# Moving the last-but-one half's outputs in a fused transformer/Mamba/recurrence kernel to other engines, with more PSUM banks for the last z projection

## The chip, the cores and the metric

One core of one Trainium2 chip runs the whole program. The metric is the device time of one execution in microseconds (us), lower is better. TensorE (PE) multiplies matrices into PSUM, VectorE (DVE), ScalarE (ACT) and GpSimd (POOL) work elementwise, and SyncE (SP) issues most of the DMAs. GpSimd reaches SBUF alone; the other two reach PSUM as well.

## The reference, cut to what matters

```python
x = x + ga * dilated_attention(adaln(x))          # layer 0
x = x + gb * fp6_ffn(adaln(x))
h = adaln(x)
x_branch, z = split(h @ in_proj_w)                # layer 1: Mamba block, D_INNER 512, 16 states
# causal conv over x_branch, silu, x_proj -> B_t, C_t, dt
for t in time: s = exp(dt*A)*s + dt*B_t*x; y = s @ C_t
x = x + ga * ((y + D*x_branch) * silu(z)) @ c_proj_w
h = adaln(x)                                      # recurrence over the BATCH index, 1024 tokens side by side
for b in 0..3: c = sig(h[b]@wf.T + c@uf.T + bf)*c + sig(h[b]@wi.T + c@ui.T + bi)*tanh(h[b]@wc.T + c@uc.T + bc)
x = x + gb * tanh(h @ wo.T + c_final @ uo.T + bo) # needs the c of the last batch
```

x is (4, 1024, 256) in float32.

## The kernel before, in words

The 4 x 1024 tokens are cut into 8 halves of 512 tokens (half 2b and 2b+1 are batch b). Each half has 32 scan steps, 256 in all: a step handles two of the 16 states of one of the four 128-channel blocks (`kd`). In a step GpSimd makes the input of the step (L1914), ScalarE two decays (L1254), VectorE the scan (L1691) and then its product with C (L1697), and TensorE adds two tiles with an identity matmul into PSUM bank Y (L874), from where VectorE takes the gated sum once per eight steps (L1677, `dve_gate`). While half h is scanned, the rest of half h-1 (z projection of the next half, c_proj, layer norm, gates, `px`) and the attention and convolution of half h+1 run between the steps.

The order on each engine is written out at build time. Every chain is a generator that yields a due time in steps (`TIMES`), and `in_time` merges the chains with the scan parts quarter by quarter; a chain part that is due comes ahead of the scan part of that quarter. After that the order in each engine's queue is fixed, and semaphores do the rest. `after(6)` is step 224, the first step of half 7.

Three places matter here. (1) **z of half 7**, steps 229 to 234: four blocks, each a matmul group (`pe_z`, L712), a tanh by ScalarE (L1142) and a product by VectorE (`dve_z`, L1421), all four through the single bank Y0; each next block's matmul waits for VectorE's product of the one before (`S.z_ev`). (2) **Outputs of the even half of all four batches**, steps 252 to 256: when half 6 has given the last c, TensorE makes `om` in banks X0 and X1 (L859). `dve_final` adds the bias (L1603) and adds `om` to the four stored `px` tiles (L1605) in the order `OUT_ORDER` = 3, 0, 1, 2; ScalarE takes four tanh (L1212), GpSimd multiplies the four by the gate row (L1887), and VectorE adds them to the four residual tiles (`dve_sum`, L1615: two behind the last scan steps, two in `dve_last`). SyncE stores each. `pe_last` makes the c_proj of half 7 for the first three channel blocks early (L747, steps 254 and 254.5); the second part uses bank X0 and so waits for the fourth `om` addition (`S.fin_add`). (3) **Behind the last scan**: `dve_gate`, last c_proj block, layer norm 4, transposes (L458), gates (L720, L728), the new c (L1639 to L1648 on VectorE), `om` of the odd halves (L784), and their outputs. `dve_last` adds the bias row to three stored tiles in that stretch (L1632).

Of the kernel before, what the change touches and what calls it, by code (L numbers as in the profile page):

```python
# [13 lines left out]
P = 128  # L14
# [88 lines left out]

OUT_ORDER = (3, 0, 1, 2)
LAST_CPROJ, LAST_GATE, LAST_PX, LAST_OM = (Y0, X0), (X1, 0, 1, 2, 3, Y), (Y0, Y), 0
# [9 lines left out]
         "modrow_step", "masks_bf", "wq_step", "wq_mm", "ffnT", "negA", "c0", "halved", "dt_mm",  # L115
         "sp_first", "first_dt", "first_row", "sums_open", "wo_gated", "ffn_gated", "cp_gated"]
ATTENTION = ["q_mm", "k_mm", "q_ev", "k_ev", "v_mm", "s_mm", "nmax", "e_ev", "rsum", "v_ev",
# [5 lines left out]
RECURRENT = ["cp_mm", "cp_tmp", "resA", "g_mm", "g_ev", "g_sig", "px_mm", "px", "c_f", "i_g", "c_new"]  # L123
END = ["om", "om_bias", "fin_add", "fin_tanh", "fin_gate_pool", "fin_gate_dve", "fin_sum", "out"]
LN = namedtuple("LN", "stats aggr step nb hn mm out")
# [13 lines left out]
def build(nc, d):  # L139
    with ExitStack() as ctx:  # L140
# [270 lines left out]
        def sp_final():  # L411
            yield after(G - 2) + 31
            for n, b in enumerate(OUT_ORDER):
                sp.wait_ge(S.fin_sum, n + 1)
                sp_out(0, b)

            sp.wait_ge(S.fin_gate_pool, B + 2)
            sp_out(1, 0)
            for n, b in enumerate((1, 2)):
                sp.wait_ge(S.fin_sum, B + n + 1)  # L420
                sp_out(1, b)
            for q in range(2):
                sp.wait_ge(S.fin_sum, B + 3 + q)
                sp.dma_start(d["out"][B - 1, TH:T, :].rearrange("(p j) e -> p j e", j=JH)[:, 2 * q:2 * q + 2, :],
                             two(xrs[1][B - 1], q)).then_inc(S.out, 16)
# [60 lines left out]
        def pe_first():  # L486
# [43 lines left out]
            for k in range(KE):  # L530
                for jo in range(2):
# [6 lines left out]
            pe.matmul(ps[:, Y, :], identF[:], wqT[:, 0:2, :, :].rearrange("p h k v -> p (h k v)"), start=True, stop=True,  # L538
                      skip_group_check=True).then_inc(S.sums_open, 1)
            pe_idle(9)  # L540
# [169 lines left out]
        def pe_z(h, kd):  # L710
            for k in range(KE):
                x = pe.matmul(ps[:, Y0, :], inw[:, k, DI + kd * P:DI + (kd + 1) * P], hB3[:, k, :],  # L712
                              start=(k == 0), stop=(k == KE - 1))
            x.then_inc(S.z_mm, 1)
# [24 lines left out]
        def pe_last():  # L739
# [11 lines left out]
            for q in range(2):  # L751

                yield t + 30 + q / 2
                if q == 0:
                    pe.wait_ge(S.gated, 4 * g + KD - 1)
                    pe.wait_ge(S.cp_gated, B)
                    pe.wait_ge(S.px, 2 * g)
                else:
                    pe.wait_ge(S.fin_add, B)
                for kd in range(KD - 1):  # L760
                    c_proj(kd, q)
# [29 lines left out]
        def pe_after(g):  # L791
# [19 lines left out]
            for kd in range(KD):  # L811
                yield t + TIMES["pe_after"]["z"][kd]
                if kd:
                    pe.wait_ge(S.z_ev, 4 * (g + 1) + kd)
                elif g >= 0:
                    pe.wait_ge(S.cp_tmp, 2 * g + 2)
                else:
                    pe.wait_ge(S.xc, 4)
                if kd == 0:
                    pe.wait_ge(ln["ln3"].out, 2 * (g + 1) + 2)  # L820
                pe_z(g + 1, kd)
# [308 lines left out]
        def act_after(g):  # L1130
# [6 lines left out]
            for kd in range(KD):  # L1137
                yield t + TIMES["act_after"]["z_tanh"][kd]
                if kd == 0 and g >= 0:
                    act.wait_ge(S.cp_mm, 2 * g + 2)  # L1140
                act.wait_ge(S.z_mm, 4 * (g + 1) + kd + 1)
                act.activation(sz[:, kd, :], ps[:, Y0, :], ACT.Tanh, scale=0.5).then_inc(S.z_tanh, 1)  # L1142
                if kd == 1 and g >= 0:
                    for j in (0, 2):
                        yield t + TIMES["act_after"]["hnA"][j // 2]
                        act.wait_ge(ln["ln4"].nb, g + 1)
                        if g:
                            act.wait_ge(S.px_out, 16 * g)
                        act_ln_rows("ln4", hnA, xrows[g % 3], g, j)
# [55 lines left out]
        def act_final():  # L1205
            for n, b in enumerate(OUT_ORDER):
                yield after(G - 2) + 29 + n / 2
                act_out(0, b, n)

        def act_out(hf, b, n):  # L1210
            act.wait_ge(S.fin_add, B * hf + n + 1)
            act.activation(pxs[hf][b], pxs[hf][b], ACT.Tanh).then_inc(S.fin_tanh, 1)  # L1212

        def act_last():
            g = G - 1
            yield STEPS * G + 1
            act.wait_ge(S.fin_sum, 1)

            act.wait_ge(ln["ln4"].nb, g + 1)
            act_ln_rows("ln4", hnA, xrows[g % 3], g, 2)  # L1220

            act.wait_ge(ln["ln4"].mm, 2 * g + 1)
            act_ln_cols("ln4", hA, LAST_CPROJ[0], 0, 8, g // 2, False)
            act.wait_ge(S.c_new, g)
            for n in range(6):
                act.wait_ge(S.g_mm, 6 * g + n + 1)
                act_gate(LAST_ORDER[n], LAST_GATE[n])

            act.wait_ge(S.g_ev, 6 * g + 6)
            act.wait_ge(ln["ln4"].out, 2 * g + 2)  # L1230
            for b in range(B):
                if b in LAST_TANH:
                    act.wait_ge(S.fin_add, B + b + 1)
# [23 lines left out]
        def act_scan(step, quarter):  # L1257
# [11 lines left out]
            if m >= 0 and m % BLOCK_STEPS == 0:  # L1269

                g, kd, i = at_step(m)
                if m:
                    act.wait_ge(S.gated, 4 * g + kd)
                else:
                    act.wait_ge(S.sums_open, 1)
                    act.wait_ge(S.halved, 1)
                act.activation(ps[:, Y, :], xc_of(g, kd), ACT.Copy, scale=vec("D", kd)).then_inc(S.dx, 1)
# [141 lines left out]
        def dve_z(h, kd):  # L1419
            dve.wait_ge(S.z_tanh, 4 * h + kd + 1)  # L1420
            dve.scalar_tensor_tensor(sz[:, kd, :], sz[:, kd, :], 1.0, ps[:, Y0, :], ALU.add, ALU.mult).then_inc(S.z_ev, 1)  # L1421

# [171 lines left out]
        def dve_final():  # L1594
            t = after(G - 2)
            om = ps[:, X0:X0 + 2, :].rearrange("p q (j e) -> p (q j) e", j=2)
            for n, b in enumerate(OUT_ORDER):
                yield t + 28.5 + n / 2
# [7 lines left out]

            yield t + 31.75
            dve_sum(0)
            yield t + 32.75
            dve_sum(1)  # L1610

        def dve_sum(n):
            b = OUT_ORDER[n]
            dve.wait_ge(S.fin_gate_pool, n + 1)
            dve.tensor_tensor(xrs[0][b], xrs[0][b], pxs[0][b], ALU.add).then_inc(S.fin_sum, 1)  # L1615

        def dve_last():
# [367 lines left out]
```

## Time and profile before

| quantity | value |
|---|---|
| median of 3 runs | 1270.52 us (1269.77 to 1271.7) |
| the profiled execution | 1271.65 us, of which 1270.1 us are the span |
| DVE busy | 1159.2 us, 91% |
| PE busy | 1145.3 us, 90% |
| POOL busy | 980.9 us, 77% |
| ACT busy | 794.3 us, 63% |

How to read it: times are microseconds from the span's start, "busy" leaves out waits on semaphores, and `[x <-ENGINE line]` on a row of the timeline is idle time of the row's engine just before it and what ended it. A duration includes time in which an instruction that has started can't get at its memory. PE counts each float32 matmul as two instructions, and the ends of matmuls are modelled: the next one starts about 0.16 us before the one ahead is shown to end.

### The profile page before, as it was taken

To read this page: it belongs to the slowest core of one execution; us is meant where nothing else is said; L and a number is where in the kernel's file an instruction comes from. 1 tells how busy PE (TensorE), PEld (TensorE's weight loads), DVE (VectorE), ACT (ScalarE), POOL (GpSimd) and SP (SyncE) were. 2 spreads that over 40 slices of the span, in tenths; PEclk is the share of its full clock that TensorE was granted. 3 is DMA by queue.
4 is the path that set the end of the run, shared out by engine and by line. 5 is a ranking of instruction groups with operands and counts; after the bars stand their busy time and mean duration, and the time that the engine had idled before them with its cause. 6 is when DMAs were issued, how large, how long until landed. Compare 5 with 4: busy or idle time off the path is not lost.

```text
span 1270.1 us, 12563 instructions
## 1 busy us (share of the span) xinstructions
PE 1145.3 (90%) x3612; PEld 641.0 (50%) x3612; DVE 1159.2 (91%) x1136; ACT 794.3 (63%) x1443; POOL 980.9 (77%) x711
## 2 busy tenths in 40 slices
PE   7989678998999899998999899998999899889896
PEld 4636333654457444764457444764457444443454
DVE  3868999999999999899999999899999999999987
ACT  2256567765785677855786678855786666645522
POOL 3216886889788988989778888989778896876852
PEclk9999989999999999999999999999999999989999
DMA  8308588876878677876768588866868686989922
GB/s 280 118 15 301 188 268 286 275 233 234 278 234 291 214 275 276 296 233 235 279 219 302 207 276 286 290 230 239 281 228 292 204 279 222 306 314 351 369 84 99
DMA packets 92308, 313.87 MB, mean 247 GB/s; under 512 B 10432, under 2 KB 15680, under 8 KB 91984
## 3 DMA queue, kind: packets, MB, share of 16 engines
q1 hardware_dynamic: 89936, 306.26, 70.1%
q10 hardware_dynamic: 2304, 6.82, 1.6%
q8 instruction: 28, 0.46, 0.1%
q14 instruction: 40, 0.33, 0.1%
HBM read 301.73 MB, written 11.31 MB: 246 GB/s over the span
## 4 chain that ended last, share of the span: by engine, by line
PE 46%; DVE 19%; POOL 16%; ACT 9%; issue 8%; DMA 2%; SPq 0%; DVEq 0%; POOLq 0%; ACTq 0%
PE ps L874 14%; DVE ps L1691 11%; POOL arena L1914 9%; PE ps L585 5%; PE ps L808 4%; PE ps L593 3%; PE ps L631 2%; DVE arena L1697 2%; PE ps L707 2%; PE ps L720 2%; PE ps L712 2%; PE ps L735 2%; ACT arena L898 2%; ACT ps L1254 2%; PE ps L728 1%
## 5 line engine op out<-in xcount | busy, mean ns | idle before, releaser
L1914 POOL TENSOR_TENSOR arena<-arena 128x1024 f32<-128x1024 f32 x255 | 600.7, 2364 | 139.9 <-PE ps L874 115.2
L1691 DVE TENSOR_TENSOR_SCAN ps<-ps,arena 128x1024 f32<-128x1024 f32 (+1 forms) x257 | 585.9, 2280 | 29.6 <-ACT ps L1254 16.7
L874 PE MATMUL ps<-arena,identF 128*128 128x512 f32 x1024 | 484.0, 604 | 46.7 <-DVE arena L1697 29.7
L1254 ACT ACTIVATE ps<-arena,negA 128x512 f32<-128x512 f32 x512 | 332.8, 684 | 89.6 <-DVE arena L1697 83.9
L874 PEld LDWEIGHTS ps<-arena,identF 128*128 128x128 f32 x1024 | 190.8, 193 | 266.6 <-issue 209.5
L1697 DVE TENSOR_TENSOR arena<-ps,arena 128x1024 f32<-128x1024 f32 x256 | 312.0, 1219 | 5.9
L889 ACT ACTIVATE arena<-arena,rnln 128x256 f32<-128x256 f32 x118 | 61.9, 590 | 42.5 <-POOL rnln L1724 25.7
L631 PE MATMUL ps<-arena,inw 128*128 128x512 f32 x128 | 60.0, 614 | 11.7 <-ACT arena L898 9.6
L712 PE MATMUL ps<-arena,inw 128*128 128x512 f32 x128 | 62.0, 608 | 3.3 <-DVE arena L1421 3.3
L1266 ACT ACTIVATE arena<-ps 128x2 f32<-128x2 f32 x128 | 22.1, 172 | 67.9 <-DVE arena L1697 67.4
L898 ACT ACTIVATE arena<-ps,modT 128x512 f32<-128x512 f32 x43 | 51.7, 1264 | 13.7 <-PE ps L458 11.6
L1733 POOL TENSOR_TENSOR arena<-arena 128x512 f32<-128x512 f32 x42 | 53.0, 1273 | 8.7 <-ACT arena L1074 7.1
L808 PE MATMUL ps<-cpw,arena 128*128 128x256 f32 x224 | 55.6, 402 | 2.1 <-DVE arena L1677 2.1
L808 PEld LDWEIGHTS ps<-cpw,arena 128*128 128x128 f32 x224 | 53.9, 327 | 5.7 <-DVE arena L1677 3.1
L585 PE MATMUL ps<-arena,wqT 128*128 128x128 f32 (+2 forms) x128 | 42.3, 481 | 12.4 <-ACT arena L898 8.1
L631 PEld LDWEIGHTS ps<-arena,inw 128*128 128x128 f32 x128 | 24.2, 194 | 45.9 <-issue 28.7
L458 PEld LDWEIGHTS ps<-identF,arena 128*128 128x128 f32 x256 | 30.1, 144 | 30.0 <-ACT arena L898 9.4
L1416 DVE SCALAR_TENSOR_TENSOR ps<-arena,vecs,ps 128x512 f32<-128x512 f32 x64 | 43.5, 749 | 0.8 <-ACT ps L1004 0.8
L458 PE MATMUL ps<-identF,arena 128*128 128x128 f32 x256 | 35.8, 280 | 6.4 <-ACT arena L898 3.6
L712 PEld LDWEIGHTS ps<-arena,inw 128*128 128x128 f32 x128 | 24.8, 195 | 31.7 <-issue 25.2
L593 PEld LDWEIGHTS ps<-wvT,arena 128*128 128x128 f32 x256 | 38.7, 227 | 3.5 <-issue 3.1
L585 PE MATMUL ps<-arena,wkT 128*128 128x128 f32 (+2 forms) x128 | 39.0, 454 | 1.0 <-ACT arena L1029 1.0
(219 smaller groups left out, 1715.7 us busy)
## 6 DMA issues: line engine op xcount, KB each, us to landing
arena<-bc_scratch SPq DMA_DIRECT2D x511, 512.0 KB, 5.0
arena<-in_x SPq DMA_DIRECT2D x16, 256.0 KB, 6.8
arena<-in_x SPq DMA_DIRECT2D x8, 512.0 KB, 8.9
xr_scratch<-arena SPq DMA_DIRECT2D x6, 512.0 KB, 6.7
px_scratch<-arena SPq DMA_DIRECT2D x6, 512.0 KB, 6.3
out_x<-arena SPq DMA_DIRECT2D x5, 512.0 KB, 2.6
arena<-bc_scratch SPq DMA_DIRECT2D x9, 256.0 KB, 3.7
woT<-in_woT SPq DMA_DIRECT2D x4, 512.0 KB, 9.4
```

Of the source, the lines that this page charges most:

```text
L458: x = pe.transpose(ps[:, bank, j * P:(j + 1) * P], src[:, j, k * P:(k + 1) * P], identF[:])
L585: x = pe.matmul(ps[:, bank, cols[0]:cols[1]], w[:, h, k, :], hB1[:, k, 0:TH:TH // (cols[1] - cols[0])], start=(k == 0), stop=(k == KE - 1))
L593: x = pe.matmul(ps[:, bank, g * P:(g + 1) * P], hB1[:, k, o * P * dil:(o + 1) * P * dil:dil], wvT[:, h, k, :], start=(k == 0), stop=(k == ...
L631: x = pe.matmul(ps[:, bank, :], inw[:, k, kd * P:(kd + 1) * P], hB3[:, k, :], start=(k == 0), stop=(k == KE - 1))
L712: x = pe.matmul(ps[:, Y0, :], inw[:, k, DI + kd * P:DI + (kd + 1) * P], hB3[:, k, :], start=(k == 0), stop=(k == KE - 1))
L808: x = pe.matmul(ps[:, Y0, (j % 2) * E:(j % 2 + 1) * E], y2T[:, kd, j:TH:JH], cpw[:, kd, :], start=(kd == 0), stop=(kd == KD - 1))
L874: x = pe.matmul(ps[:, Y, :], identF[:], inp[:, m % RING, q, :], start=False, stop=(i == BLOCK_STEPS - 1 and q == 1), skip_group_check=True)
L898: act.activation(out, src, ACT.Identity, bias=modT[:, layer_col + k, b:b + 1], scale=modT[:, layer_col + 2 + k, b:b + 1]).then_inc(ln[site ...
L1254: x = act.activation(ps[:, 2 * (m % 2) + q, :], dt[:, kd, :], ACT.Exp, scale=negA[:, kd, 2 * i + q:2 * i + q + 1])
L1691: x = dve.tensor_tensor_scan(states, states, inp[:, m % RING, q, :].rearrange("p q t -> p (q t)"), 0.0, ALU.mult, ALU.add)
L1697: dve.tensor_tensor(inp[:, m % RING, :, :], states_of(m), c_at[:, m % 3, :, :], ALU.mult).then_inc(S.prod, 1)
L1914: x = pool.tensor_tensor(inp[:, m % RING, :, :], u[:, kd:kd + 1, :].broadcast_to([P, 2, TH]), b_at[:, m % 3, :, :], ALU.mult)
```

## The change

Three edits. **z of half 7** goes through banks Y0, X1, X0, X1 (`LAST_Z`), so its matmuls no longer wait for the block before, but for the banks' former users (`S.xc`, `S.bc_sb`) and, for the fourth, for the second product (there is a count of two). Issue times of z matmuls and tanh in that half move forward (matmul of block 2 from 7.25 to 6.5; tanh from 8, 8.5, 9.25 to 7, 7.75, 9), and ScalarE's layer norm rows are issued behind the third tanh, not the second. **Outputs of the even halves**: of `OUT_ORDER` only the first `SOON` = 2 (batches 3 and 0) are made as before. ScalarE copies `om` into SBUF (`om_late`), and TensorE's early c_proj waits for this copy. GpSimd adds `om_late` for batches 1 and 2, gates both and adds both to the residual, and ScalarE takes their two tanh in `act_last`, one ahead of the layer norm rows and one ahead of the fourth gate. The sum of batch 3 goes from VectorE to GpSimd, that of batch 0 from behind the last gated product to `dve_last`. **Semaphores** are renamed and merged: `fin_gate_dve` becomes `fin_sum`, `sums_open` is gone, and ScalarE's first D product waits for `dt_mm`.

```diff
+LAST_Z = (Y0, X1, X0, X1)
-OUT_ORDER = (3, 0, 1, 2)
+OUT_ORDER, SOON, SUMS = (3, 0, 1, 2), 2, 1
+        om_late = inw[:, 1, :].rearrange("p (j e) -> p j e", e=E)
+        def z_bank(h, kd):
+            return LAST_Z[kd] if h == G - 1 else Y0
...
 def sp_final():
             for n, b in enumerate(OUT_ORDER):
-                sp.wait_ge(S.fin_sum, n + 1)
+                if n == 1:
+                    sp.wait_ge(S.fin_sum, 1)
+                else:
+                    sp.wait_ge(S.fin_pool, (1, 0, 5, 7)[n])
                 sp_out(0, b)
...
 def pe_last():
-                    pe.wait_ge(S.fin_add, B)
+                    pe.wait_ge(S.om_copy, 1)
                 for kd in range(KD - 1):
                     c_proj(kd, q)
...
 def pe_after(g):
             for kd in range(KD):
-                yield t + TIMES["pe_after"]["z"][kd]
-                if kd:
+                yield t + ((5.25, 6, 6.5, 9) if g == G - 2 else TIMES["pe_after"]["z"])[kd]
+                if g == G - 2 and kd:
+                    if kd == 1:
+                        pe.wait_ge(S.xc, 4 * G)
+                    elif kd == 2:
+                        pe.wait_ge(S.bc_sb, G)
+                    else:
+                        pe.wait_ge(S.z_ev, 4 * (g + 1) + 2)
+                elif kd:
                     pe.wait_ge(S.z_ev, 4 * (g + 1) + kd)
...
 def act_after(g):
-                yield t + TIMES["act_after"]["z_tanh"][kd]
+                yield t + ((5.75, 7, 7.75, 9) if g == G - 2 else TIMES["act_after"]["z_tanh"])[kd]
...
-                if kd == 1 and g >= 0:
+                if kd == (2 if g == G - 2 else 1) and g >= 0:
...
 def act_final():
-            for n, b in enumerate(OUT_ORDER):
+            for n, b in enumerate(OUT_ORDER[:SOON]):
                 yield after(G - 2) + 29 + n / 2
                 act_out(0, b, n)
+            yield after(G - 2) + 29.75
+            act.wait_ge(S.fin_add, SOON)
+            act.activation(om_late, ps[:, X0:X0 + 2, :].rearrange(...), ACT.Copy).then_inc(S.om_copy, 1)
...
 def act_last():
-            act.wait_ge(S.fin_sum, 1)
+            act.wait_ge(S.fin_pool, 1)
+            act_late(0)
...
             for n in range(6):
+                if n == 3:
+                    act_late(1)
                 act.wait_ge(S.g_mm, 6 * g + n + 1)
                 act_gate(LAST_ORDER[n], LAST_GATE[n])
...
+        def act_late(e):
+            b = OUT_ORDER[SOON + e]
+            act.wait_ge(S.fin_pool, 2 + 2 * e)
+            act.activation(pxs[0][b], pxs[0][b], ACT.Tanh).then_inc(S.fin_tanh, 1)
...
 def dve_final():
-            for n, b in enumerate(OUT_ORDER):
+            for n, b in enumerate(OUT_ORDER[:SOON]):
...
-            yield t + 31.75
-            dve_sum(0)
-            yield t + 32.75
-            dve_sum(1)
...
 def dve_last():
-            dve.wait_ge(S.fin_sum, 1)
+            dve.wait_ge(S.fin_pool, 1)
             dve_ln_rows("ln4", hnA, xrow, g)
...
-            dve_sum(2)
+            dve_sum(1)
...
-                if mt == 0:
-                    dve_sum(3)
...
 def pool_final():
-            for n, b in enumerate(OUT_ORDER):
+            for n, b in enumerate(OUT_ORDER[:SOON]):
                 yield after(G - 2) + 29.5 + n / 2
                 pool_out(0, b, n)
+            b = OUT_ORDER[0]
+            pool.wait_ge(S.fin_gate_pool, 1)
+            pool.tensor_tensor(xrs[0][b], xrs[0][b], pxs[0][b], ALU.add).then_inc(S.fin_pool, 1)
+            pool.wait_ge(S.om_copy, 1)
+            pool_late_add(0)
+        def pool_late_add(e):
+            x = pxs[0][OUT_ORDER[SOON + e]]
+            pool.tensor_tensor(x, x, om_late, ALU.add).then_inc(S.fin_pool, 1)
+        def pool_late_gate(e):
+            b = OUT_ORDER[SOON + e]
+            pool.wait_ge(S.fin_tanh, SOON + e + 1)
+            pool.tensor_tensor(pxs[0][b], pxs[0][b], gates1[:, b:b + 1, :].broadcast_to([P, JH, E]), ALU.mult).then_inc(S.fin_pool, 1)
+        def pool_late_sum(e):
+            b = OUT_ORDER[SOON + e]
+            pool.wait_ge(S.fin_pool, 3 + 3 * e)
+            pool.tensor_tensor(xrs[0][b], xrs[0][b], pxs[0][b], ALU.add).then_inc(S.fin_pool, 1)
 def pool_last():
             pool_power("ln4", G - 1)
+            pool.wait_ge(ln["ln4"].hn, 2 * G)
+            pool_late_gate(0)
+            pool_late_add(1)
+            pool_late_sum(0)
+            pool_late_gate(1)
+            pool_late_sum(1)
             pool_out(1, 0, 0)
```

## Rows read from the trace of the kernel before

**Rows 1.** The page's first part: busy time, share of span, instructions

```profile
PE 1145.3 (90%) x3612; PEld 641.0 (50%) x3612; DVE 1159.2 (91%) x1136; ACT 794.3 (63%) x1443; POOL 980.9 (77%) x711
```

**Rows 2.** Busy time by stretch: engine columns, then PEclk, DMA share, GB/s

```profile
1125.20:1128.98 3.78, 3.78 (x5) 1.71 (x6) 3.75 (x7) 1.30 (x2) 2.39 (x6) 0.50 1.00 377
1150.00:1205.00 55.00, 49.88 (x123) 23.90 (x122) 54.44 (x34) 27.64 (x43) 44.30 (x32) 1.00 0.98 361
```

**Rows 3.** Timeline of DVE (start, duration), z of half 7

```profile
1135.07 0.69 DVE L1421 SCALAR_TENSOR_TENSOR arena<-arena,ps 128x512 f32<-128x512 f32 x1 [2.26 <-ACT arena L1142]
1137.09 0.69 DVE L1677 TENSOR_TENSOR arena<-ps,arena 128x512 f32<-128x512 f32 x1 [0.19 <-PE ps L874]
1137.69 2.29 DVE L1691 TENSOR_TENSOR_SCAN ps<-ps,arena 128x1024 f32<-128x1024 f32 x1
```

**Rows 4.** Timeline of PE, z of half 7

```profile
1125.20 3.78 PE L712 MATMUL ps<-arena,inw 128*128 128x512 f32 x4 [3.27 <-DVE arena L1421]
```

**Rows 5.** Timeline of DVE, end of the scan

```profile
1214.82 1.21 DVE L1605 TENSOR_TENSOR arena<-arena,ps 128x1024 f32<-128x1024 f32 x1
1215.94 1.21 DVE L1697 TENSOR_TENSOR arena<-ps,arena 128x1024 f32<-128x1024 f32 x1
1225.13 2.22 DVE L1615 TENSOR_TENSOR arena<-arena 128x1024 f32<-128x1024 f32 x1
1227.62 0.69 DVE L1677 TENSOR_TENSOR arena<-ps,arena 128x512 f32<-128x512 f32 x1 [0.28 <-PE ps L874]
```

**Rows 6.** Timeline of PE, end of the scan

```profile
1207.15 7.03 PE L874 MATMUL ps<-arena,identF 128*128 128x512 f32 x16
1214.01 2.95 PE L747 MATMUL ps<-cpw,arena 128*128 128x256 f32 x12
1217.21 1.13 PE L874 MATMUL ps<-arena,identF 128*128 128x512 f32 x2 [0.25 <-DVE arena L1697]
1225.63 1.88 PE L874 MATMUL ps<-arena,identF 128*128 128x512 f32 x4
```

**Rows 7.** Timeline of POOL, end of the scan

```profile
1216.96 9.30 POOL L1887 TENSOR_TENSOR arena<-arena,rowmod 128x1024 f32<-128x1024 f32 x4
```

**Rows 8.** Timeline of DVE and of POOL where both are at SBUF

```profile
36.84 1.49 DVE L1324 TENSOR_SCALAR qsc<-amax 128x16 f32<-128x16 f32 x1
35.95 2.35 POOL L1729 TENSOR_TENSOR arena<-arena,gbias 128x1024 f32<-128x1024 f32 x1
102.29 2.80 DVE L1527 TENSOR_TENSOR arena<-arena 128x512 f32<-128x512 f32 x1
102.18 2.36 POOL L1914 TENSOR_TENSOR arena<-arena 128x1024 f32<-128x1024 f32 x1 [0.40 <-DMA arena<-bc_scratch]
104.70 2.62 POOL L1914 TENSOR_TENSOR arena<-arena 128x1024 f32<-128x1024 f32 x1 [0.16 <-DMA arena<-bc_scratch]
```

**Rows 9.** Timeline of ACT, behind the last scan

```profile
1234.68 1.09 ACT L889 ACTIVATE arena<-arena,rnln 128x256 f32<-128x256 f32 x2 [15.21 <-POOL rnln L1724]
1245.61 0.69 ACT L1177 ACTIVATE arena<-ps,vecs 128x512 f32<-128x512 f32 x1 [1.03 <-PE ps L720]
```

**Rows 10.** Timeline of DVE, behind the last scan

```profile
1238.05 1.23 DVE L1632 TENSOR_TENSOR wqT<-wqT,bias_rows 128x1024 f32<-128x1024 f32 x1
1252.20 0.69 DVE L1648 SCALAR_TENSOR_TENSOR cT<-arena 128x512 f32<-128x512 f32 x1
```

**Rows 11.** DVE's groups: busy, mean ns, idle ahead and its releaser

```profile
L1639 DVE SCALAR_TENSOR_TENSOR arena<-arena,cT 128x512 f32<-128x512 f32 x2 | 1.4, 693 | 0.6 <-ACT arena L1177 0.6
L1645 DVE SCALAR_TENSOR_TENSOR arena<-arena 128x512 f32<-128x512 f32 x2 | 1.4, 693 | 3.4 <-ACT arena L1177 3.4
```

**Rows 12.** Timeline of POOL beside two-input DVE work, and without it

```profile
47.40 1.27 POOL L1722 TENSOR_TENSOR rnln<-vnln,consts 128x4 f32<-128x4 f32 x1 [8.55 <-DVE vnln L1306]
1233.26 1.02 POOL L1722 TENSOR_TENSOR rnln<-vnln,consts 128x4 f32<-128x4 f32 x1 [7.00 <-DVE vnln L1306]
```

**Rows 13.** Timeline of PE, behind the last scan

```profile
1252.95 2.25 PE L784 MATMUL ps<-guo,cT 128*128 128x256 f32 x8 [0.38 <-DVE cT L1648]
```

More of the change, by code:

```diff
@@ L115 @@
          "modrow_step", "masks_bf", "wq_step", "wq_mm", "ffnT", "negA", "c0", "halved", "dt_mm",
-         "sp_first", "first_dt", "first_row", "sums_open", "wo_gated", "ffn_gated", "cp_gated"]
+         "sp_first", "first_dt", "first_row", "wo_gated", "ffn_gated", "cp_gated"]
 ATTENTION = ["q_mm", "k_mm", "q_ev", "k_ev", "v_mm", "s_mm", "nmax", "e_ev", "rsum", "v_ev",
@@ L123 @@
 RECURRENT = ["cp_mm", "cp_tmp", "resA", "g_mm", "g_ev", "g_sig", "px_mm", "px", "c_f", "i_g", "c_new"]
-END = ["om", "om_bias", "fin_add", "fin_tanh", "fin_gate_pool", "fin_gate_dve", "fin_sum", "out"]
+END = ["om", "om_bias", "fin_add", "fin_tanh", "fin_gate_pool", "fin_sum", "fin_pool", "om_copy", "out"]
 LN = namedtuple("LN", "stats aggr step nb hn mm out")
@@ L413, in sp_final @@
             for n, b in enumerate(OUT_ORDER):
-                sp.wait_ge(S.fin_sum, n + 1)
+                if n == 1:
+                    sp.wait_ge(S.fin_sum, 1)
+                else:
+                    sp.wait_ge(S.fin_pool, (1, 0, 5, 7)[n])
                 sp_out(0, b)
-            sp.wait_ge(S.fin_gate_pool, B + 2)
+            sp.wait_ge(S.fin_gate_pool, SOON + 2)
             sp_out(1, 0)
             for n, b in enumerate((1, 2)):
-                sp.wait_ge(S.fin_sum, B + n + 1)
+                sp.wait_ge(S.fin_sum, SUMS + 2 * n + 2)
                 sp_out(1, b)
             for q in range(2):
-                sp.wait_ge(S.fin_sum, B + 3 + q)
+                sp.wait_ge(S.fin_sum, SUMS + 5 + q)
                 sp.dma_start(d["out"][B - 1, TH:T, :].rearrange("(p j) e -> p j e", j=JH)[:, 2 * q:2 * q + 2, :],
@@ L538, in pe_first @@
             pe.matmul(ps[:, Y, :], identF[:], wqT[:, 0:2, :, :].rearrange("p h k v -> p (h k v)"), start=True, stop=True,
-                      skip_group_check=True).then_inc(S.sums_open, 1)
+                      skip_group_check=True)
             pe_idle(9)
@@ L711, in pe_z @@
             for k in range(KE):
-                x = pe.matmul(ps[:, Y0, :], inw[:, k, DI + kd * P:DI + (kd + 1) * P], hB3[:, k, :],
+                x = pe.matmul(ps[:, z_bank(h, kd), :], inw[:, k, DI + kd * P:DI + (kd + 1) * P], hB3[:, k, :],
                               start=(k == 0), stop=(k == KE - 1))
@@ L1141, in act_after @@
                 act.wait_ge(S.z_mm, 4 * (g + 1) + kd + 1)
-                act.activation(sz[:, kd, :], ps[:, Y0, :], ACT.Tanh, scale=0.5).then_inc(S.z_tanh, 1)
-                if kd == 1 and g >= 0:
+                act.activation(sz[:, kd, :], ps[:, z_bank(g + 1, kd), :], ACT.Tanh, scale=0.5).then_inc(S.z_tanh, 1)
+                if kd == (2 if g == G - 2 else 1) and g >= 0:
                     for j in (0, 2):
@@ L1205, in act_final @@
         def act_final():
-            for n, b in enumerate(OUT_ORDER):
+            for n, b in enumerate(OUT_ORDER[:SOON]):
                 yield after(G - 2) + 29 + n / 2
                 act_out(0, b, n)
+            yield after(G - 2) + 29.75
+            act.wait_ge(S.fin_add, SOON)
+            act.activation(om_late, ps[:, X0:X0 + 2, :].rearrange("p q (j e) -> p (q j) e", j=2), ACT.Copy).then_inc(S.om_copy, 1)
         def act_out(hf, b, n):
-            act.wait_ge(S.fin_add, B * hf + n + 1)
+            act.wait_ge(S.fin_add, SOON * hf + n + 1)
             act.activation(pxs[hf][b], pxs[hf][b], ACT.Tanh).then_inc(S.fin_tanh, 1)
@@ L1232, in act_last @@
                 if b in LAST_TANH:
-                    act.wait_ge(S.fin_add, B + b + 1)
+                    act.wait_ge(S.fin_add, SOON + b + 1)
                     act.activation(last_tanh(b), pxs[1][b], ACT.Tanh).then_inc(S.fin_tanh, 1)
@@ L1274, in act_scan @@
                 else:
-                    act.wait_ge(S.sums_open, 1)
+                    act.wait_ge(S.dt_mm, 1)
                     act.wait_ge(S.halved, 1)
@@ L1420, in dve_z @@
             dve.wait_ge(S.z_tanh, 4 * h + kd + 1)
-            dve.scalar_tensor_tensor(sz[:, kd, :], sz[:, kd, :], 1.0, ps[:, Y0, :], ALU.add, ALU.mult).then_inc(S.z_ev, 1)
+            dve.scalar_tensor_tensor(sz[:, kd, :], sz[:, kd, :], 1.0, ps[:, z_bank(h, kd), :], ALU.add, ALU.mult).then_inc(S.z_ev, 1)
         def dve_first():
@@ L1660, in dve_last @@
                 dve.wait_ge(S.fin_tanh, B + b + 1)
-                dve.tensor_tensor(last_tanh(b), last_tanh(b), gates1[:, b:b + 1, :].broadcast_to([P, JH, E]), ALU.mult).then_inc(S.fin_gate_dve, 1)
-                dve.wait_ge(S.fin_gate_dve, n + 1)
+                dve.tensor_tensor(last_tanh(b), last_tanh(b), gates1[:, b:b + 1, :].broadcast_to([P, JH, E]), ALU.mult).then_inc(S.fin_sum, 1)
+                dve.wait_ge(S.fin_sum, SUMS + 2 * n + 1)
                 dve.tensor_tensor(xrs[1][b], xrs[1][b], last_tanh(b), ALU.add).then_inc(S.fin_sum, 1)
-            dve.wait_ge(S.fin_gate_pool, B + 3)
+            dve.wait_ge(S.fin_gate_pool, SOON + 3)
             for q in range(2):
@@ L1896, in pool_last @@
             pool_power("ln4", G - 1)
+            pool.wait_ge(ln["ln4"].hn, 2 * G)
[4 more added lines that the diff above has]
+            pool_late_sum(1)
             pool_out(1, 0, 0)
-            pool.wait_ge(S.fin_gate_pool, B + 1)
+            pool.wait_ge(S.fin_gate_pool, SOON + 1)
             pool.tensor_tensor(xrs[1][0], xrs[1][0], pxs[1][0], ALU.add).then_inc(S.fin_gate_pool, 1)
```

## The prediction

> **What bounds the kernel now.** I read the busy shares first: VectorE 91%, TensorE 90% [rows 1]. Then the busy time by stretch: from 1150 to 1205 us VectorE works 54.44 of 55 us, so there it is the bound and GpSimd (44.3) has room [rows 2]. Only stretches where VectorE waits, or has work that another engine could take, are worth anything. The timeline shows three. At the z projection of half 7 VectorE waits 2.26 us for the third tanh and 0.19 us at the gated product after it [rows 3]; the third tanh is late because TensorE had waited 3.27 us for the first product [rows 4]. At the end of the scan VectorE has four `om` additions between the scans and two sums behind them [rows 5]. There TensorE works without a gap from 1207.15 [rows 6]. Behind the last scan the chain of waits runs through TensorE's gate matmuls, the sixth gate, the last c and the second `om` [rows 10, 13].
>
> **The change, part by part.** All positions are in time of before.
>
> *Three banks for z.* The block 1 matmuls can start at 1125.20 - 3.27 = 1121.9, where TensorE fell idle, and run at the full clock: 1.72 us in place of 3.6 (four 512-column matmuls take 1.88 with the tail; here they took 3.78 at a granted clock of 0.50, the 1.2 GHz level, right behind the 3.27 us in which TensorE stood still) [rows 2, 4, 6]. Block 2 follows one y tile later, about 1124.5 to 1126.2, and its tanh is there by 1128.5. VectorE reaches that product at 1135.07 - 2.26 = 1132.81 and no longer waits. The gated product comes next and its y matmuls, freed by the earlier z, are done at about 1131.7, so the 0.19 goes too. Gain 2.5 us. Lower bound 0, if GpSimd or the rows from DRAM pace the steps up to 1205 (DMA share 0.98 there, against GpSimd busy 44.3 of 55) [rows 2]; upper 2.6. I take 2.5: behind it VectorE hardly stands still, and the TensorE and GpSimd work that feeds it starts from VectorE's own products, so it moves along. The fourth block reuses X1 and finds its count of two products long reached. ScalarE's layer norm rows come one tanh later, and their transposes wait for the fourth product, later still.
>
> *Two `om` additions leave VectorE.* Their issue spacing is 1.12 us (1214.82 to 1215.94), so its products 254 and 255 come 2.2 us earlier [rows 5]. But TensorE can't follow. Without waits, in its own order: y 249 to 252 end at 1214.0; 12 c_proj matmuls at 0.2325 (2.79; with tail 2.95) to 1216.8; half of y 253 (0.86) to 1217.66; the second c_proj 2.79 to 1220.45; six y matmuls 2.58 to 1223.03; one gate matmul group, also four instructions of 512 columns, 1.71 to 1224.74; y 255 1.72 and tail to 1226.6. The gated product then starts at 1226.73 in place of 1227.62 [rows 5, 6]. Gain 0.9 us; bounds 0 and 2.2. The copy of `om` by ScalarE follows the second addition, which ended a scan (2.3 us) ahead of the third, at about 1212.6, and one tanh; at twice the 0.69 us of 512-wide work for each [rows 9] it is ready by 1215.4, before TensorE reaches the second c_proj at 1217.7. What is late next is TensorE, not VectorE.
>
> *The sums.* Sum 0 took 2.22 us at 1225.13, but TensorE's last y matmuls ended at 1227.51, and the gated product waited for them, so it cost nothing. The sum of batch 0 stood in a wait for c_proj; in `dve_last` it takes a place that a sum had. GpSimd's four operations from 1216.96 stay four (two gates, a sum, an addition) of 2.32 us and end at 1226.3 as before, ahead of its layer norm step [rows 7]. Nothing.
>
> *Five GpSimd operations go behind the last scan* (gate 1, add 2, sum 1, gate 2, sum 2). Their only start condition is the layer norm rows, done at 1235.77 [rows 9]. This is the costly part. When VectorE and GpSimd both read SBUF, one waits: VectorE's 512-wide product issued at 102.29 took 2.80 us and ended at 105.09, which is GpSimd's end (104.54) plus 0.55, and GpSimd's next took 2.62 for its usual 2.36. VectorE's sum at 1225.13 ended 1.09 us behind GpSimd's end at 1226.26 [rows 5, 7, 8]. A 16-wide tensor_scalar took 1.49 us under a GpSimd operation [rows 8], and GpSimd's power took 1.27 beside VectorE's three-operand work for 1.02 alone [rows 12]. So every form of VectorE work between 1238.05 and c (three bias additions, the sum, and the eight instructions for c) collides with GpSimd's reads. GpSimd's part behind 1238.05: 0.2 left of gate 1, and four more of 2.325, 9.5 us. VectorE's slack in that stretch: 0.6 + 3.4 = 4.0 us of waits for gates [rows 11], and 1.1 us because one sum has gone from it. 9.5 - 4.0 - 1.1 = 4.4 us late. Laid out instruction by instruction with the two taking turns I get the last c at 1256.9 instead of 1252.9, 4.0. I take 4.2; the bounds are 0 and 4.4. Gate 2 and sum 2 can't slip behind c: the tanh they wait for is issued behind the third gate (1246.30) and done at 1247.4 [rows 9]. That tanh sits in a 1.03 us gap of ScalarE and costs the fourth gate 0.1 us, which its next gap absorbs.
>
> The Trainium skill (SBUF — State Buffer, "Who interferes with whom") says that a VectorE instruction with two SBUF inputs, or in a 2-port mode, and a GpSimd instruction that reads SBUF shut each other out for the whole instruction. If only plain tensor_tensor did so, as the strongest rows show, four instructions would be held, the waits for gates would take it up, and this term would be about 0; by the page all twelve are held and it is the 4.2 above.
>
> *TensorE stands still ahead of `om`.* It finished the gate matmuls at 1252.95 - 0.38 - 2.0 = 1250.6 and went on with the first `om` half at once [rows 13]. Now the first c comes at about 1254.4 (four instructions, 2.5 us, ahead of the last), so it idles 3.5 us. Behind 3.27 us the clock was at 0.50 for all the next 3.78 us [rows 2, 4]. At that level each `om` half takes some 1.9 us more; the first half is mostly hidden in front of the last c. I take 1.0 us; bounds 0 and 3.2 (both halves, less what is hidden, and the start of px).
>
> *The rest.* The D product's new wait: ScalarE's softplus ahead of it already waits for `dt_mm`. SyncE's stores of these tiles end well before its last ones at 1267. Nothing.
>
> **Sum.** -2.5 - 0.9 + 4.2 + 1.0 = +1.8 us on the profiled 1271.65, so 1273.4. That execution was 1.1 us over the median, so the median goes from 1270.5 to 1272.3.
>
> **Rivals.**
> 1. *The late GpSimd work costs nothing*, because VectorE's scalar_tensor_tensor isn't held or its waits absorb it. -2.5 - 0.9 = -3.4: 1267.1. For it: VectorE has 5.1 us of slack here. Against: 9.5 us of GpSimd work against that, and the rows with waits. Chance 0.24.
> 2. *Slower: TensorE's clock stays at the lower level through `om` and into px.* Place: ahead of the first `om` half; it decides if TensorE's idle stretch there is around 3 us or more. Price 3.2 in place of 1.0: +4.0, 1274.5. Against: the first half is partly hidden. Chance 0.13.
> 3. *The z gain isn't there*, something else paces the steps to 1205: -0.9 + 4.2 + 1.0 = +4.3, 1274.8. Against: VectorE 54.44 of 55 us. Chance 0.07.
> 4. *The collision is half of it*, or VectorE gets ahead: 0 to -2: 1268.5 to 1270.5. Chance 0.06.
>
> The forecast has 0.50; its own range is 1270.8 to 1273.3. About 0.2% (2.54 us) is what a measurement of this kernel can tell from no change. Faster than that: rival 1 mostly and a little of 4, 0.25. Slower: rivals 2 and 3 and the upper edge of the forecast, 0.23. Within: 0.52. The range of 8 in 10 goes from 1266.8, just under rival 1, to 1274.6.
>
> **What would show it.** Z: VectorE's wait ahead of the third z product gone, the scan behind the gated product 2.5 us earlier, TensorE's block 1 in 1.88 us. Outputs: the last gated product 0.9 us closer to the end of TensorE's four y steps 249 to 252, still released by TensorE. Collision: L1632, L1615 or L1639 to L1648 with durations of 2 to 3.5 us, and from that gated product to the last c 29.3 us where it was 25.3. Clock: granted clock under 1 from about 1254, `om` matmuls near 4 us per eight. The prediction is wrong if those durations stay at 1.2 and 0.7 us, or if GpSimd runs its five operations where VectorE waits.

## The result and the profile after

The changed kernel takes 1273.2 us in the median (22 runs, 1270.68 to 1276.06) against 1270.49 us for the kernel before (22 runs, 1268.83 to 1272.05): a ratio of 1.002, 95% interval 1.0014 to 1.0026. By the ratio that is 2.5 us slower, by the medians 2.7. Its profiled execution took 1273.94 us, 1272.5 of them the span. The forecast was 1272.3, with a range of its own from 1270.8 to 1273.3, so the result lies just inside the upper edge.

Where the 2.4 us between the two spans lie, read from the timelines of VectorE and TensorE:

| point | before | changed | difference |
|---|---|---|---|
| start of the scan behind the gated product of step 231 | 1137.69 | 1134.89 | -2.80 |
| start of TensorE's 16 y matmuls (steps 249 to 252) | 1207.15 | 1205.44 | -1.71 |
| start of the last gated product | 1227.62 | 1225.01 | -2.61 |
| end of the last c | 1252.89 | 1253.27 | +0.38 |
| first `om` addition of the odd halves | 1255.31 | 1257.72 | +2.41 |
| end of the span | 1270.1 | 1272.5 | +2.4 |

The second column answers to [rows 3, 5, 6, 10]; the first `om` addition of before is the row below the table. So 2.6 us are won up to the last gated product, then 3.0 lost up to the last c, and 2.0 more in `om`.

```profile
1255.31 1.22 DVE L1657 TENSOR_TENSOR wqT<-wqT,ps 128x1024 f32<-128x1024 f32 x1 [2.41 <-PE ps L784]
```

VectorE at the z stage, changed kernel (timeline: start, duration, line, operation): the third z product (1132.57) starts right behind the scan, and the gated product (1134.29) waits no longer.

```profile
1124.33 0.67 DVE L1453 SCALAR_TENSOR_TENSOR arena<-arena,ps 128x512 f32<-128x512 f32 x1
1130.37 2.29 DVE L1717 TENSOR_TENSOR_SCAN ps<-ps,arena 128x1024 f32<-128x1024 f32 x1
1132.57 0.67 DVE L1453 SCALAR_TENSOR_TENSOR arena<-arena,ps 128x512 f32<-128x512 f32 x1
1134.29 0.68 DVE L1703 TENSOR_TENSOR arena<-ps,arena 128x512 f32<-128x512 f32 x1
1134.89 2.29 DVE L1717 TENSOR_TENSOR_SCAN ps<-ps,arena 128x1024 f32<-128x1024 f32 x1
```

TensorE in the changed kernel: block 1 of z takes 1.88 us and waits for nothing (answering to [rows 4]); the eight `px` matmuls take 3.13 us; `om` of the even halves waits for nothing; and `om` of the odd halves starts behind 2.93 us of idleness and takes 6.68.

```profile
1121.62 1.88 PE L724 MATMUL ps<-arena,inw 128*128 128x512 f32 x4
1194.42 3.13 PE L747 MATMUL ps<-gwo,arena 128*128 128x256 f32 x8 [2.32 <-ACT arena L1197]
1201.68 3.92 PE L879 MATMUL ps<-guo,cT 128*128 128x256 f32 x16
1205.44 7.03 PE L894 MATMUL ps<-arena,identF 128*128 128x512 f32 x16
1215.94 2.95 PE L759 MATMUL ps<-cpw,arena 128*128 128x256 f32 x12
1250.93 6.68 PE L796 MATMUL ps<-guo,cT 128*128 128x256 f32 x16 [2.93 <-DVE cT L1674]
```

The same `px` in the kernel before, at the full clock behind the same idle stretch:

```profile
1196.98 2.24 PE L735 MATMUL ps<-gwo,arena 128*128 128x256 f32 x8 [2.31 <-ACT arena L1177]
```

VectorE behind the last scan, changed kernel. Its wait for TensorE at the gated product has grown from 0.28 us [rows 5] to 4.17; two of the three 1.2 us bias additions take 3.37, and two of the instructions for c take 2.47 and 2.83 us in place of 0.43 (a row of e3 below has it) and 0.69 [rows 10, 11]. No wait for a gate is left in front of c.

```profile
1225.01 0.69 DVE L1703 TENSOR_TENSOR arena<-ps,arena 128x512 f32<-128x512 f32 x1 [4.17 <-PE ps L894]
1235.34 1.24 DVE L1660 TENSOR_TENSOR wqT<-wqT,bias_rows 128x1024 f32<-128x1024 f32 x1
1236.51 3.37 DVE L1660 TENSOR_TENSOR wkT<-wkT,bias_rows 128x1024 f32<-128x1024 f32 x1
1239.80 3.37 DVE L1660 TENSOR_TENSOR inw<-inw,bias_rows 128x1024 f32<-128x1024 f32 x1
1244.94 2.47 DVE L1669 TENSOR_SCALAR arena<-arena 128x512 f32<-128x512 f32 x1
1247.33 2.83 DVE L1671 SCALAR_TENSOR_TENSOR arena<-arena 128x512 f32<-128x512 f32 x1
1252.58 0.69 DVE L1674 SCALAR_TENSOR_TENSOR cT<-arena 128x512 f32<-128x512 f32 x1
```

GpSimd in the same stretch shows the other side of the same collisions. Its addition and first sum take 3.33 us in place of 2.36.

```profile
1233.14 2.36 POOL L1934 TENSOR_TENSOR arena<-arena,rowmod 128x1024 f32<-128x1024 f32 x1 [1.20 <-ACT arena L909]
1235.46 3.33 POOL L1929 TENSOR_TENSOR arena<-arena,inw 128x1024 f32<-128x1024 f32 x1
1238.75 3.33 POOL L1939 TENSOR_TENSOR arena<-arena 128x1024 f32<-128x1024 f32 x1
1244.60 2.52 POOL L1934 TENSOR_TENSOR arena<-arena,rowmod 128x1024 f32<-128x1024 f32 x1 [2.52 <-ACT arena L1268]
1247.20 2.40 POOL L1939 TENSOR_TENSOR arena<-arena 128x1024 f32<-128x1024 f32 x1
```

Read the two together: VectorE's second bias addition is issued at 1236.51 and ends at 1239.88, which is GpSimd's end (1238.79) plus 1.09; GpSimd's sum, issued at 1238.75, then waits for it and ends at 1242.08; VectorE's third ends 1.09 later. They take turns, one whole instruction each. Together the four held instructions of VectorE take 8.5 us more than alone (12.04 against 3.56).

Busy time by stretch, changed kernel (PE, PEld, DVE, ACT, POOL, then PEclk, DMA share, GB/s): the granted clock is 0.55 in `om`, nearly all of it at the 1.2 GHz level, right behind the idle stretch; at `px` it is 0.63.

```profile
1194.40:1198.70 4.30, 4.28 (x10) 3.24 (x11) 4.23 (x4) 1.90 (x3) 4.08 (x4) 0.63 0.90 370
1250.90:1257.60 6.70, 6.67 (x17) 5.51 (x18) 2.30 (x4) 0.00 (x0) 0.00 (x0) 0.55 0.13 53
```

### The profile page after: what moved, and what is told of

It reads as the page before. It is cut to its first block, busy times and chain, and to the rows that moved or that the text cites. A ratio compares the mean times of both kernels' runs of the same rounds, so it can differ in the third digit from the quotient of the medians.

```text
span 1272.5 us, 12563 instructions
## 1 busy us (share of the span) xinstructions
PE 1147.6 (90%) x3612; PEld 642.7 (51%) x3612; DVE 1158.4 (91%) x1131; ACT 795.3 (62%) x1444; POOL 994.3 (78%) x716
## 4 chain that ended last, share of the span: by engine, by line
PE 45%; DVE 20%; POOL 15%; ACT 9%; issue 8%; DMA 2%; SPq 0%; DVEq 0%; POOLq 0%; ACTq 0%
PE ps L894 14%; DVE ps L1717 11%; POOL arena L1968 8%; PE ps L597 6%; PE ps L820 4%; PE ps L605 3%; DVE arena L1723 2%; PE ps L747 2%; PE ps L643 2%; ACT ps L1286 2%; DMA arena<-bc_scratch 2%; ACT arena L918 2%; PE ps L719 2%; PE ps L724 1%; PE ps L629 1%
## 5 line engine op out<-in xcount | busy, mean ns | idle before, releaser
L643 PEld LDWEIGHTS ps<-arena,inw 128*128 128x128 f32 x128 | 24.2, 194 | 45.9 <-issue 28.7
L732 PE MATMUL ps<-arena,gwf 128*128 128x512 f32 x64 | 30.8, 604 | 9.6 <-ACT arena L918 9.6
```

What stands on the lines that cost most here:

```text
L643: x = pe.matmul(ps[:, bank, :], inw[:, k, kd * P:(kd + 1) * P], hB3[:, k, :], start=(k == 0), stop=(k == KE - 1))
```

## The experiments

Ratios are of a kernel's runs over those of the kernel before on the same chip, with 95% intervals. A difference in us behind a ratio is worked out from it (0.001 is 1.27 us), and can differ by some tenths from that of the medians.

**e1, z alone.** The kernel before with `LAST_Z`, `z_bank`, the waits and issue times of z, nothing else.

> The kernel before with the three banks and the new issue times for z of half 7, and nothing else of the change. Theory (the z stage is on VectorE's path, and the shift reaches the end): VectorE's scan behind the gated product comes 2.5 to 2.7 us earlier and the time falls by 1.7 to 2.6 us, to 1268 to 1269, less where TensorE's clock falls again before step 252. Rival (GpSimd or the rows from DRAM pace the steps to the end of the scan): the time stays within 0.5 us of before.

Measured: 1270.02 us, ratio 0.9987 (0.9978 to 0.9996), 1.7 us faster. That is the least of what was expected, and the median itself is above the expected 1268 to 1269. The scan behind the gated product comes at 1134.84, 2.85 us earlier, and the last gated product (step 255) at 1225.53, 2.09 earlier; the span is 2.1 us shorter. The z stage is on the path; part of its gain goes on the way (see e7 and e8).

```profile
1124.28 0.67 DVE L1434 SCALAR_TENSOR_TENSOR arena<-arena,ps 128x512 f32<-128x512 f32 x1
1225.53 0.68 DVE L1690 TENSOR_TENSOR arena<-ps,arena 128x512 f32<-128x512 f32 x1
```

**e2, outputs alone.** The changed kernel with z as before.

```diff
-LAST_Z = (Y0, X1, X0, X1)
+LAST_Z = (Y0, Y0, Y0, Y0)
...
```

The waits and issue times of before are put back as well.

> The changed kernel with z of half 7 as before: one bank, old issue times. Theory (the late GpSimd operations hold VectorE and leave TensorE idle ahead of om): 0.9 us gained at the gated product, 3.0 lost up to the last c, 1 to 2 us more in om: 3 to 4.2 us slower than before, 1273.6 to 1274.7. Rival (the loss belongs to the new banks or issue times of z): at or under before.

Measured: 1273.38 us, ratio 1.0018 (1.0008 to 1.0027), 2.3 us slower, where at least 3 were expected. The expectation had counted 1 to 2 us for `om`, and in the profile that part is missing: it has the collision (gated product to last c 28.26 us) but `om` at full clock, behind an idle stretch of the same length:

```profile
1251.70 4.64 PE L796 MATMUL ps<-guo,cT 128*128 128x256 f32 x16 [2.91 <-DVE cT L1674]
```

And it shows what the old z stage costs when TensorE's clock doesn't fall there: VectorE waits 0.49 us, not 2.26 [rows 3].

```profile
1124.51 0.67 DVE L1453 SCALAR_TENSOR_TENSOR arena<-arena,ps 128x512 f32<-128x512 f32 x1
1133.34 0.69 DVE L1453 SCALAR_TENSOR_TENSOR arena<-arena,ps 128x512 f32<-128x512 f32 x1 [0.49 <-ACT arena L1162]
1135.96 2.29 DVE L1717 TENSOR_TENSOR_SCAN ps<-ps,arena 128x1024 f32<-128x1024 f32 x1
```

```profile
1125.24 1.98 PE L724 MATMUL ps<-arena,inw 128*128 128x512 f32 x4 [3.27 <-DVE arena L1453]
```

**e3, the late GpSimd work made narrow.** Of each of the five operations one column in 256 is computed, so the outputs of the even halves of batches 1 and 2 stay incomplete. The cut below is of the sum; the gate and the second addition are made narrow in the same way.

```diff
-            pool.tensor_tensor(xrs[0][b], xrs[0][b], pxs[0][b], ALU.add).then_inc(S.fin_pool, 1)
+            x = xrs[0][b][:, :, 0:1]
+            pool.tensor_tensor(x, x, pxs[0][b][:, :, 0:1], ALU.add).then_inc(S.fin_pool, 1)
```

> The changed kernel with the five GpSimd operations behind the last scan cut to one column in 256 each; the waits, the two late tanh and everything else stay, the outputs of the first half of batches 1 and 2 are left incomplete. Theory (their time at SBUF is the loss, by VectorE's delay and by TensorE's clock): L1660 to L1674 back at 1.2, 0.7 and 0.4 us, gated product to last c 25.3 us again, om at full clock, 5 us faster than the changed kernel: 1267 to 1268.5. Rival (the late tanh, the waits or the clock by itself cost it): at most 2 us faster than the changed kernel.

Measured: 1268.0 us, ratio 0.9979 (0.997 to 0.9988). Instructions, waits and tanh are the same; without GpSimd's time at SBUF the kernel is 5.2 us faster than the changed one, and faster than before. The two intervals (this one and 1.0014 to 1.0026) lie far apart. VectorE's timeline has its durations and its waits for gates back, and c ends 25.18 us behind the gated product:

```profile
1224.04 0.69 DVE L1703 TENSOR_TENSOR arena<-ps,arena 128x512 f32<-128x512 f32 x1 [4.17 <-PE ps L894]
1235.52 1.21 DVE L1660 TENSOR_TENSOR wkT<-wkT,bias_rows 128x1024 f32<-128x1024 f32 x1
1245.09 0.43 DVE L1669 TENSOR_SCALAR arena<-arena 128x512 f32<-128x512 f32 x1
1247.80 0.69 DVE L1671 SCALAR_TENSOR_TENSOR arena<-arena 128x512 f32<-128x512 f32 x1 [2.28 <-ACT arena L1197]
1248.53 0.69 DVE L1674 SCALAR_TENSOR_TENSOR cT<-arena 128x512 f32<-128x512 f32 x1
```

**e5, the same work earlier.** Nothing is left out; both additions and one gate go into GpSimd's idle time ahead of its layer norm step, both tanh ahead of ScalarE's rows.

```diff
 def act_last():
             act_late(0)
+            act_late(1)
...
-                if n == 3:
-                    act_late(1)
...
 def pool_final():
             pool_late_add(0)
+            pool_late_add(1)
...
 def pool_last():
+            pool_late_gate(0)
             pool_power("ln4", G - 1)
...
-            pool_late_gate(0)
-            pool_late_add(1)
+            pool_late_gate(1)
             pool_late_sum(0)
-            pool_late_gate(1)
             pool_late_sum(1)
```

> The changed kernel with its GpSimd work moved: both om additions and the gate of batch 1 ahead of GpSimd's layer norm step, both tanh ahead of ScalarE's layer norm rows, so that three operations (7.0 us) and not five follow the rows. Theory: VectorE's work in the layer norm stretch reads SBUF with one operand, so it isn't held by the two operations there; behind it 4.8 us of GpSimd are left against VectorE's 5.1 us of slack: the last c at its old distance, no idle TensorE ahead of om, 1267 to 1268.5. Rival (GpSimd slows the layer norm stretch, or three operations still hold c): 1270 or more.

Measured: 1269.04 us, ratio 0.9983 (0.9974 to 0.9992). The median is above the expected 1268.5 and under the 1270 of the rival; the distance from the gated product to the last c, 25.17 us, is back as expected. The collisions are still there, but VectorE's slack covers them: the second and third bias additions take 3.36 us each, and 1.01 us of waiting for the last gate is left. In the layer norm stretch, beside a GpSimd operation, VectorE's statistics keep their 0.75 us.

```profile
1226.20 0.75 DVE L1427 BATCH_NORM_STATS2 stats_after<-arena 128x6 f32<-128x256 f32 x2
1234.90 3.36 DVE L1659 TENSOR_TENSOR wkT<-wkT,bias_rows 128x1024 f32<-128x1024 f32 x1
1247.14 0.69 DVE L1670 SCALAR_TENSOR_TENSOR arena<-arena 128x512 f32<-128x512 f32 x1 [1.01 <-ACT arena L1197]
```

```profile
1225.18 2.36 POOL L1934 TENSOR_TENSOR arena<-arena,rowmod 128x1024 f32<-128x1024 f32 x1
1233.84 6.62 POOL L1939 TENSOR_TENSOR arena<-arena 128x1024 f32<-128x1024 f32 x2
```

**e4, TensorE kept busy ahead of `om`.** The changed kernel with

```diff
+            pe.wait_ge(S.g_ev, 6 * g + 1)
+            for _ in range(3):
+                pe.matmul(ps[:, X1, :], identF[:], gw["f"][:].rearrange("p k e -> p (k e)"), start=True, stop=True, ...)
             for k in range(KE):
                 pe.wait_ge(S.c_new, g + k + 1)
```

> The changed kernel with three identity matmuls of 512 columns into a free bank between the last gate matmuls and om of the odd halves; their result is not used. Theory (the collision keeps the last c 3.0 us late, and TensorE standing still in front of om then costs up to 2.0 us more by its clock): gated product to last c stays at 28.3 us, the 16 om matmuls take at most 4.7 us in place of 6.68, and the time falls by 0.5 to 2 us to 1271.5 to 1272.7. Rival (the lower clock isn't due to the idle stretch): om still near 6.7 us, same time as the changed kernel.

Measured: 1272.51 us, ratio 1.001 (1.0001 to 1.0019), between the changed kernel and before. Taken at their middle values, 1.3 us of the 2.5 come back, but the interval overlaps that of the changed kernel (1.0014 to 1.0026), so the time doesn't tell the two apart. In its one profile `om` takes 4.64 us behind 0.35 us of idleness, and the last c is as late as ever (28.26). As `om` took 4.64 us in e2 too, without any filler, this alone doesn't show that the filler holds the clock up.

```profile
1252.67 4.64 PE L800 MATMUL ps<-guo,cT 128*128 128x256 f32 x16 [0.35 <-DVE cT L1678]
```

**Two more profiles of the changed kernel.**

> The changed kernel once more, for another profile. Theory: gated product to last c 28.3 us within 0.2, as an order of instructions gives it; the 16 om matmuls between 4.6 us (full clock) and 6.7 us, as the clock falls in some executions. Rival (the collision differs from execution to execution): the distance to the last c varies by over 1 us.

> As the run ahead of it, a third profile of the changed kernel: distance to the last c 28.3 us within 0.2, the om matmuls between 4.6 and 6.7 us.

Measured (one run each): 1273.05 and 1273.31 us. The last c ends 28.27 and 28.28 us behind the gated product, but `om` takes 4.64 us in the first and 6.76 in the second. The collision is the same in every execution seen; the clock isn't.

```profile
1252.17 4.64 PE L796 MATMUL ps<-guo,cT 128*128 128x256 f32 x16 [2.93 <-DVE cT L1674]
```

```profile
1250.31 6.76 PE L796 MATMUL ps<-guo,cT 128*128 128x256 f32 x16 [2.93 <-DVE cT L1674]
```

**e6, e7, e8: two unused matmuls ahead of `px`** of half 6, on e5, on e1 and on the kernel before.

```diff
+                    if g == G - 2:
+                        for _ in range(2):
+                            pe.matmul(ps[:, X1, :], identF[:], gw["f"][:].rearrange("p k e -> p (k e)"), start=True, stop=True, ...)
                     pe.wait_ge(S.g_ev, 6 * g + 6)
```

> The kernel with GpSimd's work moved ahead (e5_earlier) and two unused identity matmuls of 512 columns in TensorE's 2.3 us wait ahead of px of half 6. Theory (that wait is where TensorE's clock falls in some executions, in front of a stretch in which TensorE is the bound): the eight px matmuls always take 2.0 to 2.3 us, never 2.8 to 3.7, and the median is 0.3 to 1 us under e5_earlier. Rival (the clock there doesn't matter): no difference beyond 0.3 us, or slower by up to 1.7 us if the filler delays px.

> The kernel before with the z change alone (e1_z_only) and two unused identity matmuls of 512 columns in TensorE's 2.3 us wait ahead of px of half 6. Theory (z brings 2.65 us to VectorE, and a lower clock of TensorE at px takes up to 1.4 us of it back in most executions): px in 2.0 to 2.3 us, TensorE's four y steps 249 to 252 begin 2.6 to 2.9 us earlier than before, and the median is 2 to 2.8 us under before. Rival (the missing part of z's gain is lost elsewhere): as e1_z_only, 1 to 1.7 us under before.

> The kernel before with the same two unused matmuls ahead of px and nothing else: what they bring by themselves. Theory: the profile of before showed px at full clock, so at most the executions in which it fell gain; 0 to 0.7 us under before. Rival (the clock at px costs the kernel before as much as the changed one, so it says nothing on z's missing part): 0.8 us or more under before.

Measured: e6 1268.42 us, ratio 0.9977 (0.9966 to 0.9987); e7 1268.04 us, 0.9978 (0.9969 to 0.9987); e8 1270.9 us, 0.9995 (0.9986 to 1.0004). All three show the eight `px` matmuls at 2.24 us, but so do the profiles of before and of e5, without the filler. The times don't tell e6 from e5, nor e7 from e1 (their intervals overlap): with the filler, z alone gains 2.8 us (0.9978) where it gained 1.7 without (0.9987), and the filler alone gains at most 1.8 and perhaps nothing. In e7's timeline the 16 y matmuls start at 1202.09 us, 5.1 us earlier than before and not the 2.6 to 2.9 expected. Of the 3.3 us by which e7 is ahead of e1 there, 1.7 are there already at z and come from earlier.

```profile
1192.69 2.24 PE L740 MATMUL ps<-gwo,arena 128*128 128x256 f32 x8 [0.60 <-ACT arena L1194]
1202.09 7.03 PE L891 MATMUL ps<-arena,identF 128*128 128x512 f32 x16
```

What came from earlier drops out when the distance is taken inside one profile, from the first z product of half 7 to the last gated product. It shows what the clock does to the same order of instructions:

| kernel | TensorE's clock fell (lower granted clock) at | distance, us |
|---|---|---|
| before | z | 103.15 |
| e8 (before, px filler) | neither | 101.45 |
| e2 (outputs alone) | `px` | 101.27 |
| e1 (z alone) | `px` | 101.25 |
| e7 (z alone, px filler) | neither | 100.22 |
| changed | `px` | 100.68 |
| e5 | neither | 99.46 |

```profile
1126.21 0.67 DVE L1425 SCALAR_TENSOR_TENSOR arena<-arena,ps 128x512 f32<-128x512 f32 x1
1137.67 2.29 DVE L1695 TENSOR_TENSOR_SCAN ps<-ps,arena 128x1024 f32<-128x1024 f32 x1
```

(These two rows are of e8.) The two repeats, e3 and e4, where the clock fell at `px`, have 100.63 to 100.70, and e6, where it didn't, 99.75. So a fall at z cost 1.7 us in the order of before, and one at `px` 0.9 to 1.2 us in the new ones. In profiles with no fall, the z banks are worth 1.2 us and the outputs 0.5 to 0.8 more.

## Why the prediction was right, point by point

The sign, the cause (late GpSimd work that holds VectorE, then a clock loss at `om`) and the sum (+1.8 forecast, +2.5 measured) held. That the sum came this close is in part luck, for its terms were off in both directions. Forecast were 3.4 us won up to the last gated product, 4.2 lost up to the last c and 1.0 lost in `om`; the pair of profiles has 2.6, 3.0 and 2.0. The three errors (+0.8, -1.2, +1.0) leave +0.6. The forecast also gave 0.52 to a change too small to be told from none (2.54 us), and the measured one lies at that edge. The terms:

*Three banks for z* (2.5 forecast). The pair of profiles gives 2.66 (from the first z product to the scan behind the gated product 13.22 us before, 10.56 after). But two profiles without the clock drop, e2 and e8, have 11.45 and 11.46 there with the old z. So only 0.9 us belongs to the order of waits; 1.8 was TensorE's lower clock behind its 3.27 us idle stretch in that execution. The row of before showed it (PEclk 0.50), and the forecast charged it as if it were always there. Part of the gain then went at `px`: there the clock fell in the changed kernel's profile, in both repeats and in e1 to e4, in front of a stretch in which TensorE runs without a gap. The lead was 2.56 us at the start of `px` and 1.71 at the 16 y matmuls. The forecast had no such term; it took it that VectorE and what feeds it would simply move along.

*Two additions off VectorE* (0.9). From the start of the 16 y matmuls to the gated product 20.47 us before, 19.57 after: 0.90. TensorE took over as the bound there, and VectorE's wait in front of the gated product is 4.17 us. The 0.90 is against before; e1, with z alone, has 20.12, so on top of the z change the additions bring 0.55 (the two distances of 101.25 and 100.68 above say the same).

*The late GpSimd work* (4.2). It was 3.0 in all three profiles of the changed kernel and in e2 and e4 (28.26 to 28.28 us against 25.27), and it vanishes with the time of the operations alone (e3) and with their place (e5). The mis-sized part is the balance of 9.5 us against 5.1 of slack. VectorE was held for 8.5 us, not 9.5: GpSimd's four operations kept it waiting some 2.1 us each, not 2.325, and the rest of its gate ahead of them hardly at all (the first bias addition took 1.24). That leaves 3.4; the other 0.4 isn't traced further. The slack itself was right: e3 has 5.1 us of waits for gates there, the changed kernel none. The forecast's other figures for this term, 4.0 by turns and the 4.2 taken, were too large as well. Of each form that the prediction named one was held: two-input tensor_tensor (the bias additions), scalar_tensor_tensor (2.83) and the one-input tensor_scalar from SBUF to SBUF (2.47). What the Trainium skill (SBUF — State Buffer, "Who interferes with whom") says of two-input instructions and 2-port modes agrees with these durations, and the statistics of e5 (one input, 0.75 us with and without GpSimd) agree with what it says of an instruction with at most one SBUF input outside those modes, that it isn't held.

*TensorE's clock at `om`* (1.0, bounds 0 and 3.2). 2.0 us in the profiled execution and 2.1 in one repeat, 0 in the other repeat and in e2. The 1.0 lies in the middle of two outcomes, neither of which is 1.0; four profiles can't tell how often each comes, and e4's time doesn't settle it either. Rival 2, the lower clock all through `om`, is what the profiled execution shows, at 2.0 us and not 3.2.

*The sum by GpSimd, the order of the rows, the semaphores* (0). GpSimd's four operations end at 1224.5, six us ahead of its layer norm step (1230.64), and no wait in the timelines is put down to them.

The parts don't add up exactly in the medians: z alone -1.7 and outputs alone +2.3 give +0.6 where the whole has +2.5. A gap of 1.9 us is about as wide as the three intervals put together (1.8), so chance is possible but strained; how often the clock falls at z, `px` and `om` in each kernel wasn't counted, and that stays open. The rival that the late work costs nothing is refuted by e3; that the z gain isn't there, by e1, though narrowly (its interval ends at 0.9996).

The best versions, e5, e6 and e7, take 0.9977 to 0.9983 of the time before, 2.2 to 2.9 us less, and aren't told apart. e7 has no output change at all, so what the changed outputs bring even in the right place (0.5 to 0.8 us by the distances above) is within the noise of the times.

## What to carry to other kernels

Work that is handed from VectorE to GpSimd isn't off VectorE's path where VectorE works on SBUF: count GpSimd's time against VectorE's slack in the place where it lands. Better, put it beside VectorE work that kept its duration here, such as a product with one operand in PSUM or the statistics. One SBUF operand alone isn't enough: the tensor_scalar from SBUF to SBUF was held (2.47 us). A wait read from one profile can be a clock event, as 1.8 of the 2.7 us at z were: look at the granted clock of the releasing stretch, and price the wait at both levels. Where a bound engine is relieved, walk the next engine's queue instruction by instruction; here that gave the 0.9 us which the relieved engine's own 2.2 would have hidden.

## What the runs showed of the hardware

VectorE and GpSimd took turns at SBUF, an instruction each, although GpSimd's next was queued without a wait: a VectorE instruction that waits gets in at the boundary (ends 1.09 us behind GpSimd's end, twice in a row).

A product with one operand in PSUM kept its 1.2 us beside GpSimd's gates (changed kernel):

```profile
1216.15 1.23 DVE L1723 TENSOR_TENSOR arena<-ps,arena 128x1024 f32<-128x1024 f32 x1
1215.23 4.67 POOL L1913 TENSOR_TENSOR arena<-arena,rowmod 128x1024 f32<-128x1024 f32 x2
```

TensorE's clock behind an idle stretch of the same length, in the same place, fell in some executions and not in others: behind 2.9 us ahead of `om` in two profiles of four, behind 3.27 us ahead of z in the profile of before but not in e2 and e8, and behind 2.3 us ahead of `px` in seven profiles of nine (not in before and e5). At the lower level the eight `px` matmuls took 2.79 to 3.72 us in place of 2.24.
